# Hard graph attention with a residual norm on one Trainium2 core: weighted sums and merge one place later, scores behind them, eight row buffers, one copy of the turned keys

## The reference

```python
Q = (x @ WQ.T).reshape(n, HEADS, HEAD_DIM).transpose(1, 0, 2)      # K and V alike
energy = Q @ we.T + be
attn = jnp.einsum('hqd,hkd->hqk', Q, K) * SCALING + energy
attn = attn + jnp.where(adj > 0, 0.0, -jnp.inf)
attn = jax.nn.softmax(attn, axis=-1)
hard = (attn == jnp.max(attn, axis=-1, keepdims=True)).astype(jnp.float32) / HEADS
out = jnp.einsum('hqk,hkd->hqd', hard, V).transpose(1, 0, 2).reshape(n, EMBED)
return _layernorm(x + out, axis=-1)
```

## Time and profile before

| | us |
|---|---|
| median of 3 runs | 1314.79 |
| lowest and highest | 1305.92, 1315.85 |
| profiled execution, device time | 1308.77 |
| its span, first to last instruction | 1307.0 |
| mean granted TensorE clock | 0.894 of full |

### The profile page before, as it was taken

The page is one execution under the profiler, slowest core; times in us unless marked ns, Lnnn a source line. Parts: engine busy times, 40 slices in busy tenths (PEclk is TensorE's granted clock), DMA queues, the critical chain, the costliest instruction groups (busy, mean ns, idle before and its releaser), DMA issues.

```text
span 1307.0 us, 50945 instructions
## 1 busy us (share of the span) xinstructions
PE 965.9 (74%) x14758; PEld 637.3 (49%) x14759; DVE 925.6 (71%) x2616; ACT 902.7 (69%) x1688; POOL 634.1 (49%) x820
## 2 busy tenths in 40 slices
PE   4787657777777878777777777877777877877781
PEld 2343335445454545455545554555555555555451
DVE  5444537877767777767877778787777688788881
ACT  1523347778777787778777778787777787786771
POOL 0000055675656555555655556555545445555660
PEclk9988868999989898989988889898879888889995
DMA  4734468678677776877777788688778688776770
GB/s 156 226 123 156 146 196 275 203 221 271 184 249 211 234 252 194 260 235 243 226 235 240 232 259 233 213 290 273 251 249 270 208 278 271 242 237 190 223 219 33
DMA packets 89515, 290.95 MB, mean 223 GB/s; under 512 B 16985, under 2 KB 30041, under 8 KB 89497
## 3 DMA queue, kind: packets, MB, share of 16 engines
q0 software_dynamic: 48720, 199.60, 49.7%
q1 hardware_dynamic: 40776, 91.15, 20.5%
HBM read 275.98 MB, written 14.71 MB: 222 GB/s over the span
## 4 chain that ended last, share of the span: by engine, by line
PE 27%; DMA 22%; DVE 19%; issue 16%; ACT 5%; DVEq 5%; POOL 3%; POOLq 2%; SPq 1%; ACTq 1%
DMA kv<-kv_table,picks 20%; PE ps_both L1232 6%; DVE best L942 4%; PE ps_both L1141 3%; POOL kv L524 3%; PE ps_o L1244 3%; PE ps_both L1209 3%; PE ps_r L1254 3%; DVE picks L932 2%; DVE hit_vals L925 2%; ACT joined L596 2%; PE ps_both L1131 2%; PE ps_x L1194 2%; PE ps_h L1224 2%; PE ps_both L1214 2%
## 5 line engine op out<-in xcount | busy, mean ns | idle before, releaser
L524 POOL DMA_INDIRECT kv<-kv_table,picks x609 | 582.8, 957 | 477.8 <-PE ps_o L1244 329.0
L658 ACT ACTIVATE hard<-ps_both,minus_top 128x384 bf16<-128x384 f32 x402 | 212.8, 585 | 89.6 <-DVE minus_top L946 71.0
L1232 PE MATMUL ps_both<-ident_f,kv 128*128 128x128 f32 x1212 | 189.3, 297 | 96.8 <-DMA kv<-kv_table,picks 96.1
L643 ACT ACTIVATE hard_t<-ps_h 128x768 bf16<-128x768 bf16 x200 | 162.2, 811 | 128.2 <-PE ps_h L1224 122.4
L942 DVE TENSOR_REDUCE best<-ps_both 128x2 f32<-128x768 f32 x201 | 190.6, 948 | 32.6 <-PE ps_both L1214 19.9
L653 ACT COPY k_t<-ps_both 128x384 f32<-128x384 f32 x404 | 173.5, 482 | 48.3 <-PE ps_both L1232 47.7
L1209 PE MATMUL ps_both<-k_t,q_now 32*32 32x384 f32 x3216 | 200.4, 553 | 8.4 <-ACT k_t L653 6.6
L1232 PEld LDWEIGHTS ps_both<-ident_f,kv 128*128 128x128 f32 x1212 | 143.5, 152 | 114.0 <-DMA kv<-kv_table,picks 102.2
L1224 PE MATMUL ps_h<-ident_b,hard 128*128 128x128 bf16 x1200 | 109.1, 231 | 67.0 <-ACT hard L658 66.4
L1194 PE MATMUL ps_x<-pay,reached 128*128 x1224 | 121.5, 236 | 38.8 <-issue 27.5
L1214 PEld LDWEIGHTS ps_both<-mask_of,masked 128*128 128x128 bf16 x1206 | 75.7, 105 | 147.2 <-issue 147.2
(11 more groups left out here) (140 smaller groups left out, 1097.7 us busy)
## 6 DMA issues: line engine op xcount, KB each, us to landing
adj_in<-in_adj SPq DMA_DIRECT2D x128, 512.0 KB, 6.0
kv_table<-kv_out SPq DMA_DIRECT2D x32, 320.0 KB, 2.4
kv<-kv_table,picks POOLq DMA_INDIRECT x609
x_in<-in_x SPq DMA_DIRECT2D x8, 512.0 KB, 7.0
x_row<-in_x SPq DMA_DIRECT2D x32, 128.0 KB
out<-y_out SPq DMA_DIRECT2D x32, 128.0 KB
plan<-places_of SPq DMA_DIRECT2D x212, 0.0 KB
turn_flags<-flags_of SPq DMA_DIRECT2D x53, 0.0 KB
```

Source lines behind the costliest of these rows:

```text
L524: pool.indirect_dma_start(kv[m % RING][:, c, :], None, kv_table, bass.IndirectOffsetOnAxis(ap=picks[m % RING][:, c, 2:3], axis=0)).then_in ...
L643: act.activation(hard_t[m % 2][:], hard_rows_t, ACT.Copy, bias=1.0).then_inc(act_hard_t, 1)
L658: done = act.activation(hard[m % 2][:, h, :], ps_s[m % 2][h][:, 0:SLOTS], ACT.Sign, bias=minus_top[m % 2][:, h:h + 1], scale=-1.0)
L1232: mm = pe.transpose(ps_s[m % 2][h][:, c * P:(c + 1) * P], kv[m % RING][:, c, h * P:(h + 1) * P], ident_f[:])
```

## The change

The sums of item b are no longer formed at the end of PE's place b. They stand in place b+1, behind the planes and *ahead* of the scores. In a front-end turn `words`, and in a finish turn `word_step`, stand ahead of them, with their waits. DVE's merge of item b moves from the end of place b to the end of place b+1, and `keep` gets four buffers. The kv rows get eight buffers (`KVS`), four of them laid over tiles that only the set-up uses. A gather then waits for the sums of eight items before. PE's and GpSimd's bodies are written out twice because of the eight buffers. Of the tile work, `turn_rows` moves to DVE's place 1, `rows_back` to the end of PE's place 1, `norm_stats` to place 2, `row_std` to ACT's place 2 behind cast quarter 3, and `norm_rows` to DVE's place 2 behind `tops`, ahead of the merge. ACT copies the turned keys of both halves with one instruction. The casts stay where they were on ACT.

```diff
-        kv = [sb(f"kv{i}", [P, CHUNKS, ROW], F32) for i in range(RING)]
+        kv = ([sb(f"kv{i}", [P, CHUNKS, ROW], F32)[:, :, :] for i in range(KVS - len(early))]
+              + [e[:, 0:CHUNKS * ROW].rearrange("p (c w) -> p c w", c=CHUNKS) for e in early])
...
-        keep = [sb(f"keep{i}", [P, HALVES], F32) for i in range(2)]
+        keep = [sb(f"keep{i}", [P, HALVES], F32) for i in range(RING)]
...
-        def run_turns(eng, r, turn, more="more"):
+        def run_turns(eng, r, bodies, more="more"):
             with eng.Fori(0, TURNS_OUTER):
                 with eng.If_ne(r[more], 0):
-                    with eng.Fori(0, TURNS_INNER):
-                        with eng.If_ne(r[more], 0):
-                            turn()
+                    with eng.Fori(0, TURNS_INNER // len(bodies)):
+                        for turn in bodies:
+                            with eng.If_ne(r[more], 0):
+                                turn()
...
-            def gather(m, due):
+            def gather(m, due, free=True):
                 wait_alone(pool, dve_picks, due(dve_picks))
-                wait_alone(pool, pe_pv, due(pe_pv, -4))
+                if free:
+                    wait_alone(pool, pe_pv, due(pe_pv, -KVS))
                 for c in range(CHUNKS):
-                    pool.indirect_dma_start(kv[m % RING][:, c, :], None, kv_table,
+                    pool.indirect_dma_start(kv[m % KVS][:, c, :], None, kv_table,
                                             bass.IndirectOffsetOnAxis(ap=picks[m % RING][:, c, 2:3], axis=0)
-                                            ).then_inc(landed[m % RING], 16)
+                                            ).then_inc(landed[m % KVS], 16)
...
-            def keys(m, due, h):
-                act.wait_ge(pe_kt[h], due(pe_kt[h]))
-                act.copy(k_t[m % 2][:, h, :], ps_s[m % 2][h][:, 0:SLOTS]).then_inc(act_kt[h], 1)
+            def keys(m, due):
+                act.wait_ge(pe_kt, due(pe_kt))
+                act.copy(k_t[m % 2][:], ps_both[m % 2][:, :, 0:SLOTS]).then_inc(act_kt, 1)
...
-                    for h in range(HALVES):
-                        keys(b + 2, for_loop(act, r, 2), h)
+                    keys(b + 2, for_loop(act, r, 2))
...
                     if b == 2:
                         cast_quarter(3)
+                        with rows_due(act, r):
+                            row_std(tile_of(act, r, "te_done"))
                     if b == 3:
                         take_plan()
                     hards(b + 1, for_loop(act, r, 1))
@@ -695,8 +703,6 @@
                         cast_quarter(0)
                     if b == 1:
                         cast_quarter(2)
-                        with rows_due(act, r):
-                            row_std(tile_of(act, r, "te_done"))
                     act.reg_add(r["n"], r["n"], 1)
...
             def merge(m, due, group):
                 width = PARTS * HD
                 dve.wait_ge(dve_keep, due(dve_keep))
+                dve.wait_ge(pe_pv, due(pe_pv))
                 for h in range(HALVES):
                     o_run = o_all[:].rearrange("p g w -> p (g w)")[:, bass.ds(group + h * width, width)]
-                    done = dve.scalar_tensor_tensor(out=o_run, in0=o_run, scalar=keep[m % 2][:, h:h + 1],
+                    done = dve.scalar_tensor_tensor(out=o_run, in0=o_run, scalar=keep[m % RING][:, h:h + 1],
                                                     in1=ps_o[:, h * width:(h + 1) * width], op0=ALU.mult, op1=ALU.add)
-                    if h == 0:
-                        done._wait_ge(pe_pv, due(pe_pv))
                 done.then_inc(dve_merge, 1)
...
                         with rows_due(dve, r):
-                            norm_stats(tile_of(dve, r, "te_done"))
-                    if b == 0:
-                        with rows_due(dve, r):
                             odd = bits_of(dve, r["te_done"], 1)
                             with dve.If_lt(odd, 1):
-                                turn_rows(0, for_loop(dve, r, -1)(dve_merge))
+                                turn_rows(0, for_loop(dve, r, -2)(dve_merge))
                             with dve.If_ne(odd, 0):
-                                turn_rows(GPT, for_loop(dve, r, -1)(dve_merge))
+                                turn_rows(GPT, for_loop(dve, r, -2)(dve_merge))
                     if b == 2:
                         with rows_due(dve, r):
-                            norm_rows(tile_of(dve, r, "te_done"))
+                            norm_stats(tile_of(dve, r, "te_done"))
                     tops(b + 1, for_loop(dve, r, 1), listed(f"listed{b + 1}"),
                          (first_places, lambda: step_plan(dve, r), ended_places, next_places)[b])
                     if b == 0:
                         with front_end_finish(dve, r):
-                            dve.wait_ge(pe_pv, for_loop(dve, r, 0)(pe_pv))
+                            dve.wait_ge(pe_pv, for_loop(dve, r, -1)(pe_pv))
                             word_steps(fin() + 1, fin() * FIN, table())
                     if b == 3:
                         with front_end(dve, r):
-                            dve.wait_ge(pe_pv, for_loop(dve, r, 0)(pe_pv))
+                            dve.wait_ge(pe_pv, for_loop(dve, r, -1)(pe_pv))
                             words(tile_of(dve, r, "fe") * QUARTERS, tile_of(dve, r, "fe") * FIN)
                         dve.reg_add(r["fe"], r["fe"], r["fe_on"])
                         dve.reg_mov(r["fe_on"], r["fe_next"])
-                    merge(b, for_loop(dve, r, 0),
-                          dve.snap(r[f"running{b}"], min_val=0, max_val=(2 * GPT - 1) * HALVES * PARTS * HD))
+                    if b == 2:
+                        with rows_due(dve, r):
+                            norm_rows(tile_of(dve, r, "te_done"))
+                    if b > 0 or begun:
+                        merge(b - 1, for_loop(dve, r, -1),
+                              dve.snap(r[f"running{b - 1}" if b else "running_last"], min_val=0, max_val=(2 * GPT - 1) * HALVES * PARTS * HD))
                     dve.reg_add(r["n"], r["n"], 1)
...
-            run_turns(dve, r, turn)
+            turn(False)
+            run_turns(dve, r, [turn])
+            merge(RING - 1, for_loop(dve, r, -1),
+                  dve.snap(r["running3"], min_val=0, max_val=(2 * GPT - 1) * HALVES * PARTS * HD))
...
             def keys_across(m, due, uses, b):
-                pe.wait_ge(landed[m % RING], uses)
+                pe.wait_ge(landed[m % KVS], uses)
                 for h in range(HALVES):
                     for c in range(CHUNKS):
                         mm = pe.transpose(ps_s[m % 2][h][:, c * P:(c + 1) * P],
-                                          kv[m % RING][:, c, h * P:(h + 1) * P], ident_f[:])
-                    mm.then_inc(pe_kt[h], 1)
+                                          kv[m % KVS][:, c, h * P:(h + 1) * P], ident_f[:])
+                mm.then_inc(pe_kt, 1)
...
@@ -1320,38 +1330,37 @@
 
                 for b in range(RING):
                     planes_of(b + 4, for_loop(pe, r, 4), (None, finish_ranks, finish_rank_step, None)[b], f"value{b + 4}")
+                    merged = for_loop(pe, r, -1)(dve_merge, -1)
+                    if b == 0:
+                        with front_end_finish(pe, r):
+                            done = pe.snap(fin() * FIN)
+                            pe.wait_ge(dve_merge, merged)
+                            word_step(done)
+                    else:
+                        with front_end(pe, r):
+                            cast = pe.snap(fe() * QUARTERS)
+                            pe.wait_ge(dve_merge, merged)
+                            for i in ((0,), (1, 2), (3,))[b - 1]:
+                                words(cast, i)
+                    if b > 0 or begun:
+                        values(first + b - 1, for_loop(pe, r, -1))
                     scores(b + 1, for_loop(pe, r, 1))
                     hards_across(b, for_loop(pe, r, 0))
-                    if b == 2:
+                    if b == 2 and first:
                         pe.reg_add(r["uses"], r["uses"], 48)
                     if b == 3:
                         plan_made(pe, r)
                         move_back(pe, r, "value", 4)
                         load_places(pe, r, VALUES, places("value", 5))
-                    keys_across(b + 2, for_loop(pe, r, 2), r["uses"], b)
-                    merged = for_loop(pe, r, 0)(dve_merge, -1)
+                    keys_across(first + b + 2, for_loop(pe, r, 2), r["uses"], b)
                     if b == 0:
                         with front_end_finish(pe, r):
-                            done = pe.snap(fin() * FIN)
-                            pe.wait_ge(dve_merge, merged)
-                            word_step(done)
-                            flags_across(done, (act_hard_t, for_loop(pe, r, 0)(act_hard_t)))
-                    if b in (1, 2):
-                        with front_end(pe, r):
```

(23 more changed lines are left out.)

64 lines of the change are left out of this document (34 added, 30 removed).

## The result

The changed kernel takes 1501.78 us (median of 4 runs, 1498.82 to 1507.6), the kernel before 1311.89 us on the same chip (1305.92 to 1315.85). The ratio is 1.145 with a 95% interval of 1.140 to 1.150. The forecast was 1420 us with a range of 1345 to 1480: the direction was right and the size was 82 us too small, 22 us beyond the range.

A forecast was written before the change was run, and what follows sets the result against it. It took the ring buffer, gather, keys, sums as the bound, but engines' own programs in cast turns. 28 × 4.0 = +112 us, other places 0, tail +1, rounded to +112 on 1308.8: 1420 us, range 1345 to 1480.

The forecast's parts named there:

- The gathers: GpSimd's gathers: its 322.7 us wait for buffers goes, worth at most DVE's 114.4 us of waits, perhaps nothing.
- rival 4: GpSimd's own work or DVE's picks take over as the bound; plain places go to +43: 1463 us, chance 0.05.
- The plain places: The 87 places outside cast turns: gather's gain and new rings cancel, 0, between -0.5 and +0.5 us a place, ±43 us.
- The same ring: New rings in every place: merge, sums, scores, tops, 3.95 us; marks, ACT's copy, planes, sums, scores, 4.2 us.
- The three that I named: In cast turns PE waits for casts 1 to 3 us, DVE for the root about 2.4 us, delaying the merge.
- the +4.0 us for each of 28 cast turns: Each of 28 cast turns, walked at 27.9 us against 23.9 before: +4.0 us, +112 in all; ends +2.5 and +6.
- the walk of the turn: Step-by-step timing of a cast turn's four places at full clock, from the previous turn's last merge: 27.9 us.
- the turns without finish work: Turns with casts and rows but no finish work: walked at about 27.2 us, priced at +4.0 like the others.
- the pair at 46.5 us: A cast turn without finish work (27.2 us) and the pure finish turn behind it (19.3): 46.5 us.
- the tail: End of the kernel, behind the loop: one more sum and one more merge, about 1 us.
- The third rival: Half clock spreads: two or three more slow places in each cast turn, 84 us on top, 1505 us, chance 0.12.
- the sign in "What would show it": Late word reads over 31 us apart, with granted clock well below 0.89, would mean half clock was the larger cost.

## Why the prediction was right and wrong

**The gathers.** Right that the wait for buffers goes and that this is worth far less than it looks: the buffers alone gave 34 us. DVE's `picks` have become what GpSimd waits for, as rival 4 has it, but PE's 1.1 us of waiting for rows show that this holds nothing.

**The plain places.** I set them at ±0, as a gain and a ring that cancel, and this is what the runs show. In the loop's first long stretch without tile work (12 places, some 245 to 305 us) the `tops` stand 4.36 us apart on average before, 3.94 with the buffers alone and 4.22 in the changed kernel, where I worked out 4.2. Over all stretches outside the cast turns the buffers took 28 us off, and with the whole change 3 us more than before are left. The same ring also stands in the cast turns. Opened, it gave 83 us in both together.

**The waits in the cast turns.** The three that I named are there: `ps_o` for `joined` (66 times, 1.4 us each), `rstd` for `std` (26 times, 2.1 us each, against my 2.4) and the merge behind it, for which PE waits 73.3 us. The experiments confirm the cause: words later -94 us, norm later -49.

**The steps that failed** are two terms of the +4.0 us for each of 28 cast turns. Measured it was 6.7, 187 us instead of 112.

The first is the walk of the turn "at full clock". Against the turn above, from its merge at 1237.45 us: marks across at 4.2 us (my 2.9), cast 0 done at 8.3 (7.2), marks across of place 1 at 12.2 (9.8), cast 2 done at 17.4 (15.0), marks across of place 2 at 19.7 (17.8), merge at 24.3 (22.5), `tops` of place 3 at 27.6 (24.8), end at 31.0 (27.9). From step to step my durations hold within half a microsecond everywhere but in the three slow places, which took 1.3, 1.3 and 1.0 us more. One of the three needed no forecast: place 3 of the earlier trace rows has its scores at 1.53 us already, so I set a walk with no slow place against 23.9 us with one in it. (The walk also has 0.55 us for the words of place 3, one quarter, which took 0.35.) Over all 28 turns the walks (27.9 and 27.2 us) are 42 us short of what was measured (29.98 and 28.06). If the other steps hold in all of them as in the turn above, this is about what the slow places cost.

The second is that I took +4.0 also for the turns without finish work, which I "did not find a reason to price apart". I walked 27.2 us for such a turn, and measured are 28.06, near enough. But +4.0 on top of the present time means 23.2 before, and the 13 such turns took 20.20 in the trace before. My own walk meant +7.0 for them. The 15 turns with finish work took 24.35, a little over my 23.9. Together that is 32 us. The turn of pure finish work, which I walked at 19.3 us, takes 23.4, and took 23.8 before (mean of nine). That is why the pair at 46.5 us looked like no reason: measured it is 51.7, against 43.4 before.

The two make some 75 of the 82 us. The rest is the loop outside the cast turns (+3) and the tail, which gained 4 us instead of 1, with the spread of the runs.

**The third rival** at 1505 us lies 3 us from the result, and that is luck. It puts 2.5 slow places on each cast turn, and there are 2.0 (55 of 112 groups of scores), of which 0.8 were there before. It prices them at 84 us, where the walks are some 42 short. By the sign in "What would show it", a distance over 31 us between two word reads, half clock was not the larger cost either: the mean of the 13 late cast turns is 30.2 us after and 24.4 before.

That idle gaps between bursts throw the tensor engine to half clock is what the Trainium skill says (TensorE: Matmul & The Clock Gate, HAM oscillation). The trace agrees that more waiting goes with more slow scores, 55 against 22, and the filler runs show it as a cost, -30 and -21 us. It does not tell which place will be slow. In 12 turns without finish work PE stood 2.1 to 2.4 us ahead of place 1's words each time, and the scores behind them took over 1.2 us in seven and less in five. In the turn above, places 0 and 1 were slow though PE had stood no longer than 1.22 and 1.12 us at a time since the scores of the place before, and place 2 stayed fast, with 2.25 us of `rows_back` (from 1250.76 us) shortly before.

The Trainium skill's sentence on consistent bubbles (Perfetto Trace Analysis, Identifying Performance Opportunities) speaks of a gap on the engine that should be saturated, and says that it can mean too little memory. GpSimd was busy for 49% of the span. The cure by that rule gave 0.973 here, 34 us for 322.7 us of gap, and on the other kind of chip it lost (1.065).

**The account**, on the chips of 1312 us: change 1502; words later -94, 1408; norm as well -34, 1374; words and sums behind the scores as well -83, 1291; what is left of the later places, 1291 to 1278, -13 and near the edge of what the intervals tell. The last is the kernel with the buffers alone. The parts are not independent: norm alone gave 49, behind the words 34, and the half clock lies within each of them.

## What to carry to other kernels

When you walk a new order, take the time before from the same sort of turn, and at the same clock as the walk. Here one turn stood for two sorts that had taken 24.35 and 20.20 us, and it had a slow place that the walk left out. Check every sort of turn that the walk prices against the trace of before: the pure finish turn was walked at 19.3 us and had been 23.8.

Where the walk leaves TensorE standing in several places, price some of the stretches behind at its lower clock. Here 55 of 112 groups of scores ran over 1.2 us instead of 0.87, and the walks without it were some 42 us short.

Ahead of a wait that is moved to the front of an engine's queue, count what is queued behind it: the words cost 94 us not by their own 1.4 us in a turn (0.38, 0.34, 0.35 and 0.35 in the turn above), but because scores, marks and merge stood behind them. And a buffer that ends a long wait on an engine off the path is worth trying by itself, before the order is touched.

## What the runs showed that was not expected

**Multiplies for nothing made the kernel faster**, by 30 us in the change (1792 of them) and by 21 with words and norm later. In the latter only 1 of the 112 groups of scores in cast turns is slow.

**The same program differs by 19% between chips, and so does what an edit is worth.** The kernel before takes 1312 us on two chips and 1566 to 1569 us on three. The buffers alone have a ratio of 0.973 on the first kind, and 1.065 and 1.075 (1.070 to 1.079) on the second. The timeline of the buffers alone on such a chip (the run at 1682.67 us):

```profile
898.14 0.51 PE L1223 MATMUL ps_both<-mask_of,masked 128*128 128x128 bf16 x6
899.84 0.51 PE L1233 MATMUL ps_h<-ident_b,hard 128*128 128x128 bf16 x6 [1.19 <-issue]
...
903.17 0.96 DVE L951 TENSOR_REDUCE best<-ps_both 128x2 f32<-128x768 f32 x1 [2.16 <-remote]
...
906.05 0.81 ACT L652 ACTIVATE hard_t<-ps_h 128x768 bf16<-128x768 bf16 x1 [5.76 <-remote]
...
906.91 0.67 PE L1253 MATMUL ps_o<-kv,hard_t 124*32 124x96 bf16 x24 [5.49 <-ACT hard_t L652]
```

and its windows there (columns as above):

```profile
902.00:904.00 2.00, 0.00 (x0) 0.00 (x0) 0.83 (x1) 0.00 (x0) 1.58 (x2) 0.80 0.97 303
904.00:906.00 2.00, 0.00 (x0) 0.00 (x0) 0.57 (x3) 0.00 (x0) 1.19 (x2) 0.50 1.03 406
```

By its records PE had turned the marks by 900.35 us, and ACT began to copy them 5.7 us later, and the profile names nothing in between ("remote"); PE did nothing from 902 to 906, and the clock fell to 0.50 meanwhile. The durations of the engines' own instructions are the same as on the first kind (`hard_t` 810 ns on both). The ends of multiplies are modelled in these records, so they don't tell whether PE or the signal was late. What differs in these chips stays open, and so does why a longer row ring loses there. There is no trace of the kernel before on that kind.
